# Half of the attribute products of a gated graph layer formed in an earlier pass, stored in DRAM and added to by the gather itself

## The reference, cut to what matters

```python
def _L1_gnn_ref(x, edge_src, edge_dst, edge_val, weight):
    msgs = x[edge_src] * edge_val[:, None]
    agg = jax.ops.segment_sum(msgs, edge_dst, num_segments=x.shape[0])
    return agg @ weight

def _L3_gnn_ref(x, edge_index, edge_attr, W1, b1, W2, b2, Wg, bg, gamma, beta):
    src, dst = (edge_index[0], edge_index[1])
    ei = jnp.concatenate([x[src], edge_attr], axis=-1)      # 256 + 64 features
    core = jnp.maximum(ei @ W1 + b1, 0.0) @ W2 + b2
    gate = jax.nn.sigmoid(ei @ Wg + bg)
    msg = gate * core
    agg = jax.ops.segment_sum(msg, dst, num_segments=x.shape[0])
    ...                                                      # residual and layer norm
```

## Time and profile before

| | us |
|---|---|
| median of 3 runs | 4657.22 (4645.11 to 4675.9) |
| span of the profiled execution, first to last instruction | 3997.1 |
| weighted sum pass in the profile (first to last gather) | 1027.9 to 1547.4 |
| gated pass in the profile (first to last gather) | 2755.8 to 3612.4 |

### The profile page before, as it was taken

The page is one execution under the profiler, slowest core; times in us unless marked ns, Lnnn a source line. Parts: engine busy times, 40 slices in busy tenths (PEclk is TensorE's granted clock), DMA queues, the critical chain, the costliest instruction groups (busy, mean ns, idle before and its releaser), DMA issues. The chain is left out here.

```text
span 3997.1 us, 62920 instructions
## 1 busy us (share of the span) xinstructions
PE 3363.0 (84%) x19013; PEld 2751.3 (69%) x19013; DVE 2170.0 (54%) x5979; ACT 1361.6 (34%) x3888; POOL 2164.8 (54%) x2327
## 2 busy tenths in 40 slices
PE   3899995494598887696599999788999999997896
PEld 2666663263476666585599998445888888886795
DVE  7787778405555554433211113436777777777423
ACT  2777773220000000332222222114555555555231
POOL 2777776677777777676443432233444444440252
PEclk9899997697656567798799999779999999996798
DMA  7887881000333332376677875565454444441576
GB/s 233 243 221 218 221 229 31 24 1 3 107 106 105 105 106 72 94 238 195 187 246 231 255 233 179 142 143 168 143 143 143 142 143 144 143 143 60 185 211 207
DMA packets 424077, 613.66 MB, mean 154 GB/s; under 512 B 149273, under 2 KB 287650, under 8 KB 423490
## 3 DMA queue, kind: packets, MB, share of 16 engines
q1 hardware_dynamic: 310578, 327.46, 27.7%
q0 software_dynamic: 104112, 273.76, 23.8%
q10 hardware_dynamic: 9056, 8.43, 0.6%
HBM read 517.83 MB, written 91.59 MB: 152 GB/s over the span
## 5 line engine op out<-in xcount | busy, mean ns | idle before, releaser
L877 POOL DMA_INDIRECT eg_rows<-t_edge,src_i x416 | 393.4, 946 | 483.7 <-DVE eg_pre L1742 353.3
L1120 PE MATMUL ps<-sum_hot,sum_rows 128*128 128x128 f32 x1664 | 435.1, 417 | 173.5 <-DVE sum_hot L1099 91.8
L1120 PEld LDWEIGHTS ps<-sum_hot,sum_rows 128*128 128x128 f32 x1664 | 340.8, 291 | 268.0 <-DMA sum_rows<-t_row,src_i 175.1
L283 POOL DMA_INDIRECT t_cells<-times_seen,cell x416 | 413.6, 994 | 170.0 <-issue 126.2
L877 POOL DMA_INDIRECT ag_rows<-t_att,src_i x416 | 403.2, 969 | 138.1 <-issue 120.1
L877 POOL DMA_INDIRECT sum_rows<-t_row,src_i x416 | 394.0, 947 | 129.6 <-issue 118.5
L1694 PE MATMUL ps<-eg_w,eg_rT 128*128 128x256 f32 x1664 | 440.5, 387 | 0.0
L1401 PE MATMUL ps<-cv_cells,cv_high 128*128 128x384 f32 (+2 forms) x1200 | 322.7, 349 | 59.0 <-DMA cv_cells<-t_cells 59.0
L1742 DVE TENSOR_TENSOR eg_pre<-ps,eg_rows 128x512 f32<-128x512 f32 x416 | 283.5, 682 | 129.2 <-PE ps L1681 123.2
L1694 PEld LDWEIGHTS ps<-eg_w,eg_rT 128*128 128x128 f32 x1664 | 284.8, 191 | 56.1 <-issue 34.1
L1401 PE MATMUL ps<-cv_cells,cv_low 128*128 128x384 f32 (+2 forms) x1200 | 309.2, 338 | 8.2 <-POOL cv_low L1364 8.2
(11 more groups left out here) (420 smaller groups left out, 6471.7 us busy)
## 6 DMA issues: line engine op xcount, KB each, us to landing
cv_cells<-t_cells SPq DMA_DIRECT2D x225, 384.0 KB, 3.7
cv_cells<-t_cells SPq DMA_DIRECT2D x75, 448.0 KB, 4.2
xn<-in_L_ffn_W SPq DMA_DIRECT2D x57, 512.0 KB
t_cells<-zeros SPq DMA_DIRECT2D x17, 1664.0 KB, 8.1
xn<-in_L_ffn_expert_w SPq DMA_DIRECT2D x110, 256.0 KB, 3.8
ag_trow<-t_dst SPq DMA_DIRECT2D x104, 256.0 KB, 3.7
t_cells<-zeros POOLq DMA_DIRECT2D x8, 1664.0 KB
eg_eaT<-in_edge_attr SPq DMA_DIRECT2D x208, 64.0 KB, 3.2
```

The lines of the kernel that those rows point to most:

```text
L283: nc.gpsimd.indirect_dma_start(out=t_cells, out_offset=bass.IndirectOffsetOnAxis(ap=cell[:, c:c + 1], axis=0), in_=times_seen[:, c:c + 1], ...
L877: nc.gpsimd.indirect_dma_start(out=rows[:, j, :], out_offset=None, in_=table, in_offset=bass.IndirectOffsetOnAxis(ap=src_i[:, n:n + 1], ax ...
L1120: mm = nc.tensor.matmul(ps[:, j % BANKS, k * EC:(k + 1) * EC], lhs, hot[:, j, :], start=True, stop=True)
```

## The change

In the weighted sum pass PE now also forms the attribute products of the first pair (two chunks) of each lot, eight instructions a lot of the shape that line 1681 has, into PSUM banks 6 and 7. ACT copies the two banks (128 x 1024 numbers) to `kept`, a ring of four, and SP stores them in a new DRAM table `t_pre`, 512 KB a lot. The pass's own products go round six banks, not eight. SP loads the weights (four transfers, which PE waits for at the start) and one pair of attributes a lot.

In the gated pass the "early" chunks (the first two of each lot) take another path. SP loads their stored products (512 KB a lot, rows of 4 KB) into `early`, four lots deep, when the lot four before has its last early message done. POOL gathers the node rows of an early chunk with `compute_op=ALU.add`, so that the transfer adds them to what lies in `early`. PE, ACT and DVE read `early` directly once that transfer has landed: there is no `gpre` for these chunks. The "late" chunks (the last two of a lot) go the way of before, with a ring of eight row buffers for them alone. POOL's queue holds, for each lot, a wait for the loaded products, two adding gathers, a wait for `gpre`, and two plain gathers. On SP the load of stored products stands behind the attributes of the same lot, and the wait for it ahead of the attributes of the next.

```diff
@@ edge_pass @@
+            w1g = sb(tag + "_w1g", [2 * ATTR, 2 * D], F32, c)
+            eaT = sb(tag + "_eaT", [2 * ATTR, ER, EC], F32, c)
+            kept = sb(tag + "_kept", [EC, KEPT, 2, 2 * D], F32, c)
-            BANKS = 8
+            BANKS, AB = 6, 6
...
+                @block.sync
+                def _(sp):
+                    attribute_weights(sp, w1g, g.loaded)
+                    for l in range(NL + 2):
+                        if l < NL:
+                            if l >= ER:
+                                sp.wait_ge(g.pre_ready.sem, g.pre_ready.at(2 * (l - ER) + 2))
+                            attributes_in(sp, eaT, l, 0)
+                        if l >= 2:
+                            sp.wait_ge(g.hid_done.sem, g.hid_done.at(l - 1))
+                            sp.dma_start(early_rows(l - 2), kept[:, (l - 2) % KEPT]).then_inc(slot_stored[(l - 2) % KEPT].sem, 16)
...
+                @block.scalar
+                def _(act):
+                    for l in range(NL):
...
+                        act.wait_ge(g.pre_ready.sem, g.pre_ready.at(2 * l + 2))
+                        nc.scalar.copy(kept[:, l % KEPT], ps[:, AB:AB + 2, :]).then_inc(g.hid_done.sem, 1)
...
                 @block.tensor
                 def _(pe):
...
+                    pe.wait_ge(g.loaded.sem, g.loaded.at(16 * 4))
+                    for n in range(NCH):
+                        j = n % GR
+                        if n % ER == 0:
+                            if n > 0:
+                                pe.wait_ge(g.hid_done.sem, g.hid_done.at(n // ER))
+                            attribute_products(pe, w1g, eaT, n // ER, AB, g.pre_ready)
+                        pe.wait_ge(gath[j].sem, gath[j].at(16 * (n // GR) + 16))
                         pe.wait_ge(g.one_hot.sem, g.one_hot.at(n + 1))
-                        if not (first and j < BANKS):
+                        if n >= BANKS:
                             pe.wait_ge(g.added.sem, g.added.at(1 + n - BANKS + 1))
@@ edge_gated @@
             rows = sb("eg_rows", [EC, GE, 2 * D], F32, c)
+            early = sb("eg_early", [EC, ER, 2, 2 * D], F32, c)
...
-            pre = sb("eg_pre", [EC, GE, 2 * D], F32, c)
+            sums = sb("eg_pre", [EC, ER, 2 * D], F32, c)
...
-                    gathers(pool, t_edge, rows, GE, g.gpre_done, beside=offset)
+                    for n in range(NCH):
+                        o, l = late_number(n), n // ER
+                        if late(n):
+                            if o >= GE and o % 2 == 0:
+                                pool.wait_ge(g.gpre_done.sem, g.gpre_done.at(o - GE + 2))
+                            nc.gpsimd.indirect_dma_start(out=rows[:, o % GE, :], out_offset=None, in_=t_edge,
+                                                         in_offset=bass.IndirectOffsetOnAxis(ap=src_i[:, n:n + 1], axis=0)).then_inc(landed(n)[0].sem, 16)
+                        else:
+                            if n % ER == 0:
+                                pool.wait_ge(early_in[l % ER].sem, early_in[l % ER].at(16 * (l // ER) + 16))
+                            nc.gpsimd.indirect_dma_start(out=early[:, l % ER, n % 2, :], out_offset=None, in_=t_edge,
+                                                         in_offset=bass.IndirectOffsetOnAxis(ap=src_i[:, n:n + 1], axis=0),
+                                                         compute_op=ALU.add).then_inc(landed(n)[0].sem, 16)
+                        offset(n)
...
-                    for m in range(ER, PAIRS):
-                        sp.wait_ge(g.pre_ready.sem, g.pre_ready.at(2 * (m - ER) + 2))
-                        attributes_in(sp, eaT, m)
+                    for l in range(ER, NL):
+                        sp.wait_ge(g.pre_ready.sem, g.pre_ready.at(2 * (l - ER) + 2))
+                        attributes_in(sp, eaT, l, 1)
+                        sp.wait_ge(g.msg_done.sem, g.msg_done.at(2 * (ER * (l - ER) + 1) + 2))
+                        early_products_in(l)
...
                     def gpre(n, i, j, first):
-                        s = j
-                        dve.wait_ge(g.pre_ready.sem, g.pre_ready.at(n + 1))
+                        if not late(n):
+                            return
+                        o = late_number(n)
+                        dve.wait_ge(g.pre_ready.sem, g.pre_ready.at(o + 1))
```

More of the change, by code:

```diff
@@ L203, in build_in @@
     slot_stored = [sig(f"slot_stored{j}") for j in range(8)]
+    early_in = [sig(f"early_products_in{j}") for j in range(ER)]
     wload = [sig(f"weights{e}") for e in range(8)]
@@ L1075, in att_pass, with attribute_weights, attributes_in, attributes_passed @@
             s.passed(NL)
+    ATTR = 64
+    KEPT = 4
+    def attribute_weights(sp, w1g, loaded):
+        for h in range(2):
+            sp.dma_start(w1g[h * ATTR:(h + 1) * ATTR, 0:D], io["L3_gnn_W1"][D:D + ATTR, :]).then_inc(loaded.sem, 16)
+            sp.dma_start(w1g[h * ATTR:(h + 1) * ATTR, D:2 * D], io["L3_gnn_Wg"][D:D + ATTR, :]).then_inc(loaded.sem, 16)
+    def attributes_in(sp, eaT, l, pair):
+        sp.dma_start(eaT[:, l % ER, :], io["edge_attr_64"][bass.ds(2 * l + pair, 1)].rearrange("m p e -> p (m e)")).then_inc(attr_in[l % ER].sem, 16)
+    def attributes_passed():
+        for j in range(ER):
+            attr_in[j].passed(16 * ((NCH // ER - j + ER - 1) // ER))
+    def attribute_products(pe, w1g, eaT, l, bank, ready):
+        pe.wait_ge(attr_in[l % ER].sem, attr_in[l % ER].at(16 * (l // ER) + 16))
+        for c in range(2):
+            for h in range(2):
+                r = slice(h * ATTR, (h + 1) * ATTR)
+                mm = nc.tensor.matmul(ps[:, bank + h, c * D:(c + 1) * D], eaT[r, l % ER, :], w1g[r, c * D:(c + 1) * D], start=True, stop=True)
+                if c == 1:
+                    mm.then_inc(ready.sem, 1)
+    def early_rows(l):
+        return t_pre[EC * l:EC * (l + 1), :].rearrange("p (h f) -> p h f", h=2)
     def edge_pass(tag, table, weight):
@@ L1107, in add @@
                             f = featT[:, :, bass.ds(b, EC)]
-                            nc.vector.tensor_tensor(f, f, ps[:, (ER * h + j) % BANKS, 0:KD * EC].rearrange("p (k t) -> p k t", k=KD), ALU.add).then_inc(g.added.sem, 1)
+                            nc.vector.tensor_tensor(f, f, ps[:, n % BANKS, 0:KD * EC].rearrange("p (k t) -> p k t", k=KD), ALU.add).then_inc(g.added.sem, 1)
                     steps(dve, NL, LOTS, [(LOTS - 1, one_hots), (0, add)])
@@ L1119, in body @@
                             lhs = rows[:, j, k * 128:(k + 1) * 128]
-                            mm = nc.tensor.matmul(ps[:, j % BANKS, k * EC:(k + 1) * EC], lhs, hot[:, j, :], start=True, stop=True)
+                            mm = nc.tensor.matmul(ps[:, n % BANKS, k * EC:(k + 1) * EC], lhs, hot[:, j, :], start=True, stop=True)
                         mm.then_inc(g.agg_ready.sem, 1)
[L1122 to L1128, removed]
         gathers_passed(GR)
         g.agg_ready.passed(NCH), g.one_hot.passed(NCH), g.added.passed(1 + NCH)
+        g.loaded.passed(16 * 4), g.pre_ready.passed(2 * NL), g.hid_done.passed(NL), attributes_passed()
+        for j in range(KEPT):
+            slot_stored[j].passed(16 * ((NL - j + KEPT - 1) // KEPT))
     def turn_back(extra_rows):
```

73 lines of the change are left out of this document (43 added, 30 removed).

## The result

The change takes 4548.06 us against 4658.55 (medians of four runs each), a ratio of 0.9765 with an interval of 0.9747 to 0.9784: 110 us less, where 103 were forecast. So the 660 us between them are a difference of chips and lie inside the span.

What follows compares the result with a forecast made beforehand. The prediction took coupled PE and DVE to bound the gated pass, with PE alone after the change, and POOL to pace the sum pass. Its terms, -112 + 4 + 3 + 2 = -103 us, gave 4554 us from 4657; range 4515 to 4720.

Steps and rivals of the forecast that it cites:

- The 660 us outside of the span: Whole kernel: span 3997.1 us against a median of 4657.22; the rest left unchanged, so a difference of spans equals one of times.
- The lot: Gated pass: four chunks fall from 8.33 to 7.25 us on PE, -112 us over 104 lots (-83 to -147).
- the stretch comes from DVE being late: Gated pass: reason for expecting the last chunk at 1.53 us instead of 1.81, since DVE gets more slack than PE.
- The 0.33 behind them: Gated pass: 0.33 us in which PE's loads wait after the attribute products, kept in the forecast lot.
- Start: Gated pass: the first gather waits for a 512 KB load, shifting all that follows by +4 us (3 to 7).
- The sum pass: Sum pass: more DMA traffic slows gathers by up to 9 us, taken as +3; PE's and ACT's added work is covered.
- The last store's +2: End of the sum pass: the last store lands some 2 us after the last addition, +2 us (0 to 5).
- up to 1.8 times: Gated pass: likeliest DMA price of an adding gather relative to a plain one, with nothing put in the sum.
- rivals 1 and 2: Gated pass: DMA engines become the bound, 4621 us (chance 0.18); or adding gathers make it slower, 4770 us (chance 0.20).
- Rival 3: Sum pass: PE at 1.2 GHz becomes the bound, 0.3 us a lot or +33, 4587 us; chance 0.10.
- Rival 4: Gated pass: early rows come late, waits move from `gpre` to the transfer, lot stays at 8.3, 4665 us; chance 0.05.
- POOL's issue: Gated pass: issuing an adding gather takes 0.95 to 1.9 us, so POOL needs 5 to 6.9 us a lot, under 7.25.

Runs made afterwards that it cites:

- e1: The kernel before, unedited, run again for a profile on a fast chip: 3994.93 us, beside 3994.59 for the comparison's own runs.
- e10: The changed kernel with a ring of eight stored products instead of four, on a fast chip: 3909.96 us against 3994.25 for the kernel before, ratio 0.9777.
- e11: The kernel before, unedited, on a slow chip: 4726.42 us, ratio 1.0009.
- e5: The changed kernel, unedited, run again on a slow chip: 4582.45 us against 4722.24 for the kernel before, ratio 0.9703.
- e12: The changed kernel with a ring of eight stored products instead of four, on a slow chip: 4587.95 us against 4726.86 for the kernel before, ratio 0.9714.
- e8: The changed kernel with each 512 KB early load also made into a tile nobody reads: 4594.55 us, 12 more than the changed kernel on that chip.
- e6: The changed kernel with the gated pass's attribute products one chunk later in PE's queue: 4589.66 us, 7 more than the changed kernel on that chip.
- e7: The changed kernel with the gated pass's attribute products as 128-row products against zero-padded weights: 4637.9 us against 4582.45 for the changed kernel.
- e2: The gated pass as changed, the sum pass as before, early loads reading other rows: 3908.95 us against 3994.59 for the kernel before, ratio 0.9796.
- e4: The changed kernel with early gathers plain, overwriting the stored products instead of adding: 3910.88 us, ratio 0.9796 to the kernel before.

## Why the prediction was right, and where it wasn't

The stretches of the profiled executions tell where the time went. Each is taken from a first and a last start of PE's loads. "Ahead of it" is all up to the last load of `cv_high` in the long stage before the gated pass (L1401 of before), and holds the sum pass. "Start" is from there to the first transpose. "Steady" is from there to the last aggregation load.

```
                       ahead of it   start    steady    sum     time (medians)
fast: e1 (before)      2470.0        287.4    868.9
      e10 (ring of 8)  2472.6        293.3    775.3
      difference       +2.6          +5.9     -93.6     -85     -84
slow: e11 (before)     3099.4        317.1    932.0
      e5 (the change)  3109.6        326.4    775.9
      difference       +10.2         +9.3     -156.1    -137    -140
```

e5 and e11 ran on two slow chips; e12, on e11's own, gives +8.3, +7.5 and -155.8. What lies ahead of the gated pass differs by up to 14 us among e5 to e8 on one chip, with the sum pass's gathers at 612 us in all four, so the +10.2 lies within that spread.

- **The 660 us outside of the span, which "I leave as they are",** were a false reading of two numbers from two chips. The decision drawn from it, to work from the span's rows, gave the gain of a fast chip and added it to the time of a slow one. Of the timed runs only the times were at hand, without their spans, so the two readings couldn't be told apart then; a gap of 660 us ought to have been kept as an open question and not as a constant.
- **The lot** was forecast at 7.25 us and is 7.41 (0.73 + 0.33 + 4 x 1.53 + 0.23; -96 us instead of -112). The step that failed is "the stretch comes from DVE being late": 0.20 of it comes with the 64-row products, as e6 and e7 show, and stays. The 0.33 behind them stays too, as forecast. Of the stretch of 0.28 in the last chunk only 0.05 to 0.08 were DVE's.
- **On a slow chip the lot of before is longer,** since its `gpre` comes late there. That is the 62 us that the steady stretch gains beyond a fast chip. The prediction had coupled PE and DVE, as is right, but at the slack of one chip. It is the likeliest reason that the result is -110 and not -84. That is argued and not shown, for no profile of the kernel before was taken on the result's chip. The profile of the changed kernel there has the start (326.3 us) and the steady part (775.9) of e5, and is 34.7 us shorter ahead of them. The kernel before is 64 us faster there than beside e5. By my estimate the other 29 us are then a steady stretch of before that was that much shorter, and with it the gain.
- **DVE** has its slack: it waits 117.3 us for PE in 88 lots, and PE is 100% busy. PE became the only bound, as forecast.
- **Start:** +4 (3 to 7) was forecast, and it is +5.9 on a fast chip, inside the bounds, and +9.3 on a slow one. In the changed kernel it is 12.6 us from SP's issue of the first load of stored products to the first transpose (3388.64 to 3401.23).
- **The sum pass** was forecast at +3, and is +2 on a fast chip, 4 to 10 on a slow one (606 and 612 us against 602; only the 612 of e12 is from the chip of the 602). The last store's +2 doesn't show apart from it.
- **DMA:** "up to 1.8 times" was the range taken for a gather that adds; it is 1.6 to 1.8. The share was forecast at 0.78 at plain prices and reads 0.90. That a share of 1 would be the bound, on which rivals 1 and 2 stood with 0.38 of the chance, is refuted by e8. The Trainium skill, DMA: Bandwidth & Descriptors, "Where 436 GB/s comes from", had spoken for more room (435 GB/s of the fabric, about 358 of HBM). The trace agrees in the direction, with 289 GB/s in e8 against 221 in the changed kernel; neither ceiling was reached by a run here.
- **Rival 3** (PE at 1.2 GHz bounds the sum pass) was wrong in its sign: the clock rose with the added work, to 1.00 on a fast chip and from 0.71 to 0.78 and 0.81 on slow ones. **Rival 4** was wrong: PE waits for no DMA in the steady stretch.
- **POOL's issue** of a gather that adds is 1.56 us, inside the bounds of 0.95 to 1.9, and hidden.

So the mechanism was right (PE alone bounds the gated pass, the adding gathers and the early path are hidden), and the method's -103 us stands against -84 where its rows came from. That it came so near to -110 was luck: a term too large by 16 us and a chip on which the old coupling costs more pulled in opposite directions.

## What to carry to other kernels

Before a difference of spans is used, set the profiled execution's span and clock beside those of the timed runs: here they differed by 2 us on the same chip and by 660 on two. Where two engines are coupled with 0.1 us of slack, a change that frees the second one can be worth more on a chip on which that slack is gone. Price a DMA share by loading it further (e8) and not by how near it reads to 1, and count 64-row products with 0.5 us around every block of them, as measured here.

## What the runs showed of the hardware

- The same program takes 3995 us on one chip and 4727 on another, with the same packets and bytes (424077 and 613.66 MB).
- A gather that adds takes 1.6 to 1.8 times the DMA share of a plain one for the same bytes (if the plain ones beside it keep their price) and POOL 1.56 us instead of 0.95 to 0.99, yet its whole cost here was within 2 us (e2 and e10 against e4).
- A DMA share of 1.03 is possible at 289 GB/s, with PE 99.8% busy.
- A block of 64-row products between 128-row ones costs PE 0.20 us ahead of it and 0.33 behind; eight 128-row products take 1.60 us where eight 64-row ones take 0.73.
- On a fast chip PE's clock in the sum pass went from 0.64 to 1.00 when products were added to it, and the median load of the unchanged work from 333 to 192 ns; on slow chips the clock read 0.71 before and 0.78 to 0.81 after.
